# Attention scores over two halves of the partitions, transposed and plain products in turn

## What is computed

```python
qg = x @ Wq + bq
Q, gate = (qg[..., :D], qg[..., D:])
K = x @ Wk + bk
V = x @ Wv + bv
Q = _rmsnorm(Q, qn_w)          # per head, 8 features
K = _rmsnorm(K, kn_w)
scores = jnp.einsum('bhqd,bhkd->bhqk', Q, K) / jnp.sqrt(jnp.float32(HD))
attn = jax.nn.softmax(scores.astype(jnp.float32), axis=-1).astype(Q.dtype)
out = jnp.einsum('bhqk,bhkd->bhqd', attn, V)
out = out * jax.nn.sigmoid(gate)[..., None]
return out @ Wo + bo
```

## Time and profile before

| | us |
|---|---|
| median of 3 runs | 1137.25 |
| lowest and highest of them | 1133.21, 1138.63 |
| the profiled execution | 1129.86 |
| its span | 1128.2 |

### The profile page before, as it was taken

One profiled execution on the slowest core, in us unless ns is written; L12 is line 12 of the kernel. 1 busy time (PEld: TensorE's weight loads), 2 busy tenths in 40 slices (PEclk: granted clock), 3 DMA queues, 4 the chain that ended last, 5 costly groups with the idle time before them and its releaser, 6 DMA issues. The chain is left out here.

```text
span 1128.2 us, 26188 instructions
## 1 busy us (share of the span) xinstructions
PE 675.7 (60%) x5838; PEld 432.4 (38%) x5839; DVE 741.2 (66%) x2260; ACT 536.6 (48%) x1335; POOL 584.1 (52%) x940
## 2 busy tenths in 40 slices
PE   2477887878888788788888888761356660000000
PEld 0134555545545445454455555430345550000000
DVE  5486998898898898889888889634622222333333
ACT  1255876677777777677677777640022220000000
POOL 4121456555655655665565655556222226666765
PEclk9588999899999998999999999965599995555555
DMA  2245545344544544545454453310666563333333
GB/s 60 62 127 130 128 116 143 93 114 113 133 110 106 137 113 104 128 104 124 109 124 110 113 133 99 86 43 28 227 201 203 204 194 90 98 102 94 106 98 95
DMA packets 115825, 132.72 MB, mean 118 GB/s; under 512 B 16901, under 2 KB 96613, under 8 KB 115269
## 3 DMA queue, kind: packets, MB, share of 16 engines
q1 hardware_dynamic: 96036, 91.93, 32.0%
q0 software_dynamic: 12736, 33.84, 9.4%
q10 hardware_dynamic: 7008, 6.43, 2.0%
HBM read 78.62 MB, written 52.96 MB: 117 GB/s over the span
## 5 line engine op out<-in xcount | busy, mean ns | idle before, releaser
L1144 DVE TENSOR_REDUCE negmax<-mx_ps 128x2 f32<-128x512 f32 x512 | 340.2, 684 | 77.6 <-remote 41.0
L892 ACT ACTIVATE pr<-st_ps 128x512 f32<-128x512 f32 x512 | 286.7, 597 | 51.3 <-PE st_ps L1536 45.5
L1514 PE MATMUL mx_ps<-k_aug,q_aug 126*128 126x256 bf16 x1024 | 203.4, 283 | 74.4 <-DVE negmax L1144 58.2
L1536 PE MATMUL st_ps<-q_aug,k_aug 128*128 128x256 bf16 x1024 | 176.6, 281 | 0.9 <-ACT pr L892 0.3
L1550 PE MATMUL o_ps<-pr,v_aug 128*32 128x256 f32 x2048 | 141.2, 394 | 48.0 <-ACT oT L898 25.9
L781 POOL DMA_INDIRECT yg<-ys_d,gi x128 | 124.3, 971 | 63.1 <-issue 41.1
L713 POOL DMA_INDIRECT xs_d<-h,slot x128 | 127.7, 998 | 55.6 <-DVE slot L1267 32.0
L1514 PEld LDWEIGHTS mx_ps<-k_aug,q_aug 126*128 126x128 bf16 x1024 | 77.0, 99 | 176.8 <-issue 168.2
L1536 PEld LDWEIGHTS st_ps<-q_aug,k_aug 128*128 128x128 bf16 x1024 | 96.5, 103 | 35.1 <-issue 11.8
L1550 PEld LDWEIGHTS o_ps<-pr,v_aug 128*32 128x32 f32 x2048 | 56.8, 110 | 98.1 <-issue 78.1
L1416 DVE TENSOR_SCALAR yw<-yg,p_all 128x128 f32<-128x128 f32 x64 | 16.1, 310 | 113.1 <-DMA yg<-ys_d,gi 87.4
(11 more groups left out here) (188 smaller groups left out, 1317.5 us busy)
## 6 DMA issues: line engine op xcount, KB each, us to landing
q_aug<-q_d SPq DMA_DIRECT2D x64, 192.0 KB
ys_d<-ys POOLq DMA_DIRECT2D x48, 256.0 KB, 3.0
mod_o<-mod_d SPq DMA_DIRECT2D x32, 256.0 KB
bias_p<-bias_d SPq DMA_DIRECT2D x32, 200.0 KB
q_d<-parts SPq DMA_DIRECT2D x32, 192.0 KB, 2.1
k_d<-parts SPq DMA_DIRECT2D x32, 192.0 KB, 2.1
k_aug<-k_d SPq DMA_DIRECT2D x64, 96.0 KB
xs<-xs_d ACTq DMA_DIRECT2D x48, 128.0 KB, 2.2
```

What stands on the lines that cost most here:

```text
L892: nc.scalar.activation(pr[:, h % PR], st_ps[score_bank(b, h)][:], ACT.Exp, scale=SCALE).then_inc(exp_d, 1)
L1144: v.tensor_reduce(negmax[:, :, h], mx_ps[h % 2][:], AX.X, ALU.max, negate=True).then_inc(mx_d, 1)
L1514: last = t_.matmul(mx_ps[h % 2][:, qc], q_aug[b.par][0:MROW, h, qc * P:(qc + 1) * P], k_aug[b.par][0:MROW, h, :], start=True, stop=True)
L1536: last = t_.matmul(st_ps[score_bank(b, h)][:, kc], k_aug[b.par][:, h, kc * P:(kc + 1) * P], q_aug[b.par][:, h, :], start=True, stop=True)
```

## The change

**What it does.** The 48 rows of a head fit in half of the partitions. Even heads now lie on partitions 0 to 49, odd ones on 64 to 113 (48 rows and 2 for the maxima), so that q_aug and k_aug are half as wide (8 heads, not 16) and nothing between needs zeros; both fills go. A plain head contracts over 48 rows of its half, a transposed one over 50. `scores_kq(bk, hk, bq, hq)` issues a transposed head of one half and a plain head of the other as four products in turn: transposed, plain, transposed, plain. It first waits for everything that either of the two needs, and both semaphores are raised at the end. Where one of the two batches doesn't exist, the head runs alone as before.

The order of `step` on TensorE is written anew: 14 pairs, with transposed 13 and 14 and plain 1 and 2 alone. The other tasks stay in their sequence but stand between other heads.

k_d in memory has six rows and not three, so SyncE stores the parts of k in three pieces, 384 KB a batch and not 192, in turn with those of q. Each half of the heads is still loaded by four transfers, now of 48 rows of 2 KB each. The maxima are written by two transfers of 16 rows and not one. The head order inside negmax, msplit and v_aug is even heads first (`head(h)`); VectorE's denominator and gated_out read and write with one more dimension for it, in as many instructions.

```diff
-MROW = P - 2
+HALF = P // 2
@@ SyncE
                 for a, n in enumerate(TERMS):
                     sp.dma_start(q_d[b.par, row:row + n]...broadcast_to([P, n, NT])).then_inc(parts_st, 16)
+                    sp.dma_start(k_d[b.par, row:row + n]..., parts[:, 1, 0:n]).then_inc(parts_st, 16)
                     row += n
-                sp.dma_start(k_d[b.par].rearrange("a p t -> p a t"), parts[:, 1]).then_inc(parts_st, 16)
...
-                sp.dma_start(q_aug[b.par][MROW:MROW + 2], mrows[:]).then_inc(mrow_ld, 16)
+                for f in range(2):
+                    sp.dma_start(q_aug[b.par][f * HALF + ROWS:f * HALF + ROWS + 2], mrows[f * H:(f + 1) * H]).then_inc(mrow_ld, 16)
@@ VectorE, start
-            for i in range(2):
-                v.memset(q_aug[i][:], 0.0).then_inc(aug_z, 1)
@@ TensorE
+            def q_waits(b, h):
                 if h % (H // 2) == 0:
                     wait(pe, aug_ld[b.par][h // (H // 2)], 64 * (b.nth + 1))
                 wait(pe, mx_d, H * b.n + h - 1)
+            def score_q(b, h, qc):
+                rows = slice(h % 2 * HALF, h % 2 * HALF + ROWS)
+                return t_.matmul(mx_ps[h % 2][:, qc], q_aug[b.par][rows, h // 2, qc * P:(qc + 1) * P],
+                                 k_aug[b.par][rows, h // 2, :], start=True, stop=True)
...
+            def scores_kq(bk, hk, bq, hq):
+                if bk is None or bq is None:
+                    scores_k(bk, hk)
+                    scores_q(bq, hq)
+                    return
+                k_waits(bk, hk)
+                q_waits(bq, hq)
+                pe.nop(nofuse=True)
+                for c in range(TB):
+                    last_k = score_k(bk, hk, c)
+                    last_q = score_q(bq, hq, c)
+                last_k.then_inc(st_r, 1)
+                last_q.then_inc(mps_r, 1)
@@ TensorE, step
-                scores_k(b3, 3)
-                scores_q(b2, 5)
+                scores_kq(b3, 3, b2, 6)
                 transpose_qk(b1)
...
```

More of the change, by code:

```diff
@@ L162, in build @@
         rest = sb("rest", [P, 2, NT])
-        q_aug = [sb(f"q_aug{i}", [P, H, NT], BF16) for i in range(2)]
-        k_aug = [sb(f"k_aug{i}", [P, H, NT], BF16) for i in range(2)]
+        q_aug = [sb(f"q_aug{i}", [P, H // 2, NT], BF16) for i in range(2)]
+        k_aug = [sb(f"k_aug{i}", [P, H // 2, NT], BF16) for i in range(2)]
         negmax = sb("negmax", [P, TB, H])
-        msplit = sb("msplit", [P, TB, 2, H])
+        msplit = sb("msplit", [P, TB, 2, 2, H // 2])
         mlead = sb("mlead", [P, TB, H], BF16)
@@ L1522, in transpose_max, with k_waits, score_k @@
                 for qc in range(TB):
-                    last = t_.transpose(bank[0:2 * H, qc * P:(qc + 1) * P], msplit[:, qc].rearrange("p a h -> p (a h)"), ident[:])
+                    last = t_.transpose(bank[0:2 * H, qc * P:(qc + 1) * P], msplit[:, qc].rearrange("p f a i -> p (f a i)"), ident[:])
                 last.then_inc(mT_ps, 1)
+            def k_waits(b, h):
+                if isinstance(b.n, int) and b.n == 0 and h == 0:
+                    pe.wait_ge(ones_ld, 64)
+                if h == 0:
+                    wait(pe, mrow_ld, 32 * (b.n + 1))
+                wait(pe, exp_d, H * b.n + h + score_bank_read(b, h))
+            def score_k(b, h, kc):
+                rows = slice(h % 2 * HALF, h % 2 * HALF + ROWS + 2)
+                return t_.matmul(st_ps[score_bank(b, h)][:, kc], k_aug[b.par][rows, h // 2, kc * P:(kc + 1) * P],
+                                 q_aug[b.par][rows, h // 2, :], start=True, stop=True)
             @of_batch
             def scores_k(b, h):
-                if isinstance(b.n, int) and b.n == 0 and h == 0:
-                    pe.wait_ge(ones_ld, 32)
-                if h == 0:
-                    wait(pe, mrow_ld, 16 * (b.n + 1))
-                wait(pe, exp_d, H * b.n + h + score_bank_read(b, h))
+                k_waits(b, h)
                 pe.nop(nofuse=True)
                 for kc in range(TB):
-                    last = t_.matmul(st_ps[score_bank(b, h)][:, kc], k_aug[b.par][:, h, kc * P:(kc + 1) * P],
-                                     q_aug[b.par][:, h, :], start=True, stop=True)
+                    last = score_k(b, h, kc)
                 last.then_inc(st_r, 1)
+            def scores_kq(bk, hk, bq, hq):
[11 more added lines that the diff above has]
+                last_q.then_inc(mps_r, 1)
             @of_batch
```

117 lines of the change are left out of this document (53 added, 64 removed).

## The result

| | kernel before | changed kernel |
|---|---|---|
| median of 4 runs, us | 1137.94 | 1344.63 |
| lowest and highest | 1133.21, 1139.79 | 1340.54, 1349.36 |
| ratio | | 1.1825, interval 1.1768 to 1.1883 |
| span of the profiled execution | 1128.2 | 1340.2 |

207 us slower, where 64 were forecast, and outside the range. The sign was right, the size was not.

The account below looks back on a forecast made before the run. VectorE was taken to bound the kernel through its work and stops. Stops of 2.16 us a step in 30 steps gave 65 us, the start -1, so 1137 + 64 = 1201 us; range 1165 to 1232.

Parts of the forecast that it names:

- What bounds the kernel: Attention and routing steps: VectorE bounds, a step costing its work (18.6 of 21.2 us) plus the moments it stands still.
- Pair and tiling change: TensorE's score products: a pair takes 0.22 us, not 0.44; each change between whole and split array costs 0.09 us.
- Rival C: Much slower: pairs run in turn or each tiling change takes 0.27 us; both 1266 us, one about 1233; chance 0.12.
- Stops (1) to (3): New VectorE waits each step before the remainder, the second denominator and maximum 14: 0.8, 0.66 and 0.7 us.
- (3): VectorE waits for maximum 14, behind the late second probability product, the counts and plain head 14: 0.7 us a step.
- Later in the step ... I put zero there.: Rest of the step, order close to the old: zero, with 0.2 us possible loss or up to 0.6 gain.
- The granted clock may be low more often; a dip costs 1 to 2 us. I leave it to the range.: TensorE's clock may dip more often as engines idle more: 1 to 2 us a dip, covered only by the range.
- path terms: TensorE durations summed on the path to the second denominator, including probability product 1.00 us and output transposes 0.60 us.
- (2): VectorE waits for the output transpose before its second denominator: path 3.10 us against 2.44, a 0.66 us stop.
- The remote stop as a fixed cost: Once a step, before the maxima of heads 0 and 1, VectorE stands still 1.98 us; taken as unchanged.
- Transfers: SyncE's six stores start loads about 1.0 us later: zero in steady steps, 1.0 us a step if uncovered.

Follow-up runs that it names:

- e7_spread: The kernel before with GpSimd's scatters that stand together near the end of a step spread apart; 1.0731 times the kernel before, on a free chip.
- e6_rows: The kernel before without multiplying the zero rows (48 and 50 rows, all in the lower half); four runs from 1170.5 to 1285.6 us, beside 1051.9.

## Why the prediction was wrong, point by point

- **What bounds the kernel.** Right. VectorE's work stayed at 18.6 to 19.3 us a step on average in every kernel but `e7_spread` (20.5), and the differences were in its stops. The exception is in `e6_rows`: in its steps at half clock TensorE bounds.
- **Pair and tiling change.** Right: 0.23 us a pair, 0.09 us a change. Rival C, pairs in turn, did not occur at full clock, although C's time (1233 to 1266) was nearer than the forecast.
- **Stops (1) to (3).** Right in place and releaser, but for (3), which stands before the ranks; the prediction said that the ranks add nothing. With whole-array products on a held chip they measure 9.2, 14.5 and 6.5 us in 12 steps, so 0.77, 1.21 and 0.54 us a step, 2.5 together for 2.16; on a free chip 0.75, 0.84 and 0.5.
- **"Later in the step ... I put zero there."** This step failed by a size. The order costs 25.2 - 21.6 = 3.6 us a step on a held chip, not 2.16: beside the 2.5 that leaves 1.1 before the maxima, the squares, the Newton steps and the residual. At full clock it costs 2.7, so most of what the sum missed in the order went with the clock too. As a whole 103 us instead of 64. In the changed kernel the projection comes late as well, 1.1 us a step, where the prediction put 0.2 as a possible price and then zero.
- **"The granted clock may be low more often; a dip costs 1 to 2 us. I leave it to the range."** This is the step that failed. The clock was read as something that happens to a kernel from time to time. It is largely a result of the change: 0.96 before, 0.79 with the halves alone, 0.65 with both. The halves were priced at zero and cost 95 us alone and 104 on top of the order. The path terms (product 1.00, transposes 0.60) were sizes at full clock; as lengths in the profile they went from 1.07 and 0.60 to 1.93 and 1.11. That alone brings (2) from 0.66 to 2.03 us, of 2.44 measured; how the rest splits was not taken apart. The range, up to 1232 us, allowed for dips of 1 to 2 us, where the period is 5.7 us over the forecast in every step.
- **The remote stop as a fixed cost.** Right for a held chip: ScalarE's copy still waits for it, and VectorE's stop moved to maximum 1 (1.54 us, by TensorE). But it depends on the chip and not on the kernel alone: none on free chips, where the order's ratio is the same (1.0902 and 1.0904) and the changed kernel's lower (1.1637 for 1.1825). Its clock differs too, 0.80 for 0.65 with the same products; why is not shown.
- **Transfers.** Priced at zero. On free chips TensorE waits about 1 us a step for `k_aug` in the changed kernel (11.5 us in 300) and in the order run with the old layout (14.2), and on held chips hardly at all (none in the changed kernel). With the new stores and the old order it is 5.1 us in 500 on a free chip, so most of it comes with the order. How much of it reaches VectorE was not separated.

What stays open: what exactly lowers the clock. Shown is that rows and time both move it, with the order and the layout kept (zero rows in and out, pairs once and twice); not shown is by what rule, and the doubled pairs with zero rows did not reach the clock of the order run. The chip moves it as well. Open too is what holds TensorE's results on some chips.

## What to carry to other kernels

Zero rows in a product can be worth their place. They cost no time here (at full clock a plain head of two products lasts 0.38 to 0.39 us with 126 rows and with 48), and without them TensorE's granted clock fell and everything else on it took longer. Before an edit that makes TensorE's work smaller, work out the path once more with every TensorE duration taken from a stretch at half clock (here the second window of the earlier trace rows had such stretches), and give that result a chance of its own. And an order in lockstep moves every product that others wait for; put those ahead of the pairs. Two of them, moved back ahead, were worth 26 us.

## What was not expected of the hardware

- With the same instructions in the same order, the granted clock fell from 0.96 to 0.79 when 48 to 50 of 128 rows were fed instead of 126 to 128, while TensorE's modelled busy share rose from 83% to 89%, partly because the same products last longer at the lower clock. It stood still 87 us of 500 before, 3.1 us at the longest, and 54 us with the halves, 2.0 at the longest. The Trainium skill ("TensorE: Matmul & The Clock Gate", HAM oscillation) ties the fall of the clock to gaps in which TensorE is idle. Here the gaps became fewer and shorter as the clock fell, and `e6_rows` has steps at half clock without a gap, by the modelled ends; the measurement decides: how full the array is counts as well.
- Two products in different halves start within 0.03 us of each other, and the next two follow 0.12 us later, about as after a single one of whole arrays (0.11).
- The same kernel takes 8% longer on two of the four chips than on the others (1137 against 1052 us). The stop of some 2 us a step that the profile calls remote was in every trace of the one kind and in none of the eight of the other.
